# Graph network kernel: count units of 30 columns instead of 40, edge attributes copied to PSUM by ScalarE and summed from there, the last two stages begun with count group 0

## The reference

```python
# stages 0 and 1: edge attributes are used, batch norm follows
msg = relu(x[src] + edge_attr)                 # 100000 x 128
agg = segment_sum(msg, dst, num_segments=6250)
h = (x + agg) @ W1l + b1l
h = relu((h - mean(h)) * rsqrt(var(h) + 1e-5) * gl + bl)
x = relu(relu(h @ W2l + b2l))
# stages 2 and 3: no attributes
agg = segment_sum(x[src], dst, num_segments=6250)
h = relu(((1 + eps) * x + agg) @ wA.T + bA) @ wB.T + bB     # relu after stage 2 only
```

## Time and profile before

| what | before |
|---|---|
| median of 3 runs | 2944.27 us |
| profiled execution | 2942.28 us, span 2939.8 us |
| gathers of stage 0, first to last | 48.5 to 1063.0 us |
| gathers of stage 1 | 1117.6 to 2140.5 us |
| stage 2, first gather to first product of the perceptron | 2214.7 to 2547.9 us |
| stage 3, the same | 2580.8 to 2913.3 us |
| busy: PE, DVE, ACT, POOL | 1875.7, 1610.4, 519.3, 2024.0 us |

### The profile page before, as it was taken

How to read it: one execution, slowest core, us unless ns; L and a number is a source line. 1 busy time by engine, 2 the same in 40 slices (tenths; PEclk the granted TensorE clock), 3 DMA queues, 4 the chain that set the end, 5 groups by cost and what they waited for, 6 DMA issues and landing times.

```text
span 2939.8 us, 28632 instructions
## 1 busy us (share of the span) xinstructions
PE 1875.7 (64%) x9233; PEld 1286.7 (44%) x9233; DVE 1610.4 (55%) x1943; ACT 519.3 (18%) x584; POOL 2024.0 (69%) x2060
## 2 busy tenths in 40 slices
PE   2555465555555564565655555555566999969998
PEld 2434343444444342343434343344343566535665
DVE  6656666665666544666666666665654222342222
ACT  3111111111111222111222222222252000120001
POOL 3777777777777736777777777777706777267772
PEclk8777777777787777788788788988887999979999
DMA  5333333334343423344444444444405666266663
GB/s 166 101 114 109 114 111 105 122 100 128 108 130 110 133 75 109 124 135 122 137 133 139 130 140 136 161 138 154 128 28 189 215 216 215 81 198 205 217 217 100
DMA packets 224848, 403.61 MB, mean 137 GB/s; under 512 B 41225, under 2 KB 129117, under 8 KB 224741
## 3 DMA queue, kind: packets, MB, share of 16 engines
q1 hardware_dynamic: 159204, 267.94, 26.3%
q0 software_dynamic: 65536, 134.35, 17.0%
HBM read 337.92 MB, written 64.21 MB: 137 GB/s over the span
## 4 chain that ended last, share of the span: by engine, by line
POOL 53%; PE 24%; issue 17%; DVE 3%; DMA 1%; ACT 1%; SPq 1%; DVEq 0%; POOLq 0%; ACTq 0%
POOL xg L532 53%; PE psA L1210 16%; PE psG L1225 4%; PE psG L1274 2%; PE psA L1282 1%; DMA cell_room<-count_store 1%; DVE hid L927 0%; ACT rows_h L580 0%; PE psG L1189 0%; DVE xp_room L933 0%; SPq L411 0%; PE psG L1304 0%; PE psA L1291 0%; DVE xp_room L737 0%; DVE rows_h L766 0%
## 5 line engine op out<-in xcount | busy, mean ns | idle before, releaser
L532 POOL DMA_INDIRECT xg<-node_table,src_all x1568 | 1560.0, 995 | 576.6 <-issue 477.4
L1189 PE MATMUL psG<-hid,xp_room 128*128 128x160 f32 x3136 | 658.2, 389 | 793.3 <-DVE hid L820 793.3
L1189 PEld LDWEIGHTS psG<-hid,xp_room 128*128 128x128 f32 x3136 | 635.0, 265 | 836.6 <-issue 836.6
L552 POOL DMA_INDIRECT xg<-node_table,idx x480 | 460.9, 960 | 286.0 <-issue 275.4
L845 DVE TENSOR_SCALAR cell_room<-psG,cell_all 128x1960 f16<-128x1960 int16 x544 | 630.1, 1218 | 0.0
L856 DVE TENSOR_TENSOR xp_room<-xp_room,xg 128x1024 f32<-128x1024 f32 x196 | 238.7, 1218 | 670.4 <-DMA xg<-node_table,src_all 670.3
L1174 PE MATMUL psA<-cell_room,xp_room 128*128 128x512 f16 (+1 forms) x2176 | 478.4, 370 | 145.1 <-ACT count_out L590 145.1
L1174 PEld LDWEIGHTS psA<-cell_room,xp_room 128*128 128x128 f16 x2176 | 206.6, 98 | 386.4 <-ACT count_out L590 180.1
L590 ACT CAST count_out<-psA 128x1960 f16<-128x1960 f32 x96 | 172.0, 1792 | 960.6 <-PE psA L1174 960.6
L595 ACT ACTIVATE xp_room<-xp_room 128x1024 f32<-128x1024 f32 x196 | 206.3, 1057 | 722.2 <-DVE xp_room L856 721.8
L1210 PE MATMUL psA<-cell_room,xp_room 128*128 128x480 f16 x1200 | 248.9, 369 | 56.9 <-DMA cell_room<-count_store 56.9
(11 more groups left out here) (128 smaller groups left out, 611.6 us busy)
## 6 DMA issues: line engine op xcount, KB each, us to landing
xp_room<-in_edge_attr_dram SPq DMA_DIRECT2D x98, 768.0 KB, 4.7
cell_room<-count_store SPq DMA_DIRECT2D x16, 3000.0 KB
count_store<-count_out SPq DMA_DIRECT2D x96, 490.0 KB, 3.1
hid<-count_store SPq DMA_DIRECT2D x16, 2880.0 KB, 11.4
xp_room<-in_edge_attr_dram SPq DMA_DIRECT2D x98, 256.0 KB, 5.1
xg<-node_table,src_all POOLq DMA_INDIRECT x1568, 2.5
node_table<-rows_h SPq DMA_DIRECT2D x48, 256.0 KB, 2.3
xg<-node_table,idx POOLq DMA_INDIRECT x480
```

Of the source, the lines that this page charges most:

```text
L532: nc.gpsimd.indirect_dma_start(xg[:, n % 2, u, j, :], None, table, bass.IndirectOffsetOnAxis(ap=src_all[:, s, j:j + 1], axis=0),).then_inc ...
L552: nc.gpsimd.indirect_dma_start(xg[:, q, u, j, :], None, table, bass.IndirectOffsetOnAxis(ap=idx[:, q, u, j:j + 1], axis=0),).then_inc(row_ ...
L1189: last = nc.tensor.matmul(psG[:, q, h * WIN:(h + 1) * WIN], ea[:, t, u, j, :], hot[:, q, u, j, :], start=(u == slots[0] and j == 0), stop= ...
```

## The change

- `CW` is 30, with 0.8 in place of 0.9 in the rule that sizes the units. By `unit_sizes()` this gives 136 units (8 groups of 17) instead of 96; `cells` has 1470 columns, `psA` is used in three banks (512, 512, 446), a group's product has 17*30 = 510 columns. The ring of cells has eight entries.
- The freed bank of `psA` is `ea_stage`, room for one super's attributes (512 columns). ScalarE copies the attributes of each super there, and VectorE adds `xg` to them from there, super by super (four adds of 512 columns in a turn), writing to `ea` as before. ScalarE stages super i+1 once super i is summed.
- ScalarE's evictions of a turn (`units_out`) now stand between the ReLU of half 0 and the wait for super 2 of that turn; before, they stood ahead of both halves.
- Gathers count on a semaphore for each super.
- In stages 2 and 3 TensorE multiplies both halves of group 0 first, then window 0, and from there half 0 of the next group, window, half 1, window. VectorE and ScalarE follow that order. SyncE loads half 0 of group 0 ahead of the table's stores.

```diff
-CW = 40
+CW = 30
-            if NODES * (b * b - a * a) + 1 + 0.9 * sqrt((n + 1) * P) / degree > CW - 1:
+            if NODES * (b * b - a * a) + 1 + 0.8 * sqrt((n + 1) * P) / degree > CW - 1:
-UPG = 12
+UPG = 17
-CELL_RING = 6
+CELL_RING = 8
+        ea_stage = psA[:, 3, 0:EPP * D]
@@ sync
+            load_half(2, 0, 0)
+            store_table(2)
             load_counts(2)
+            load_half(3, 0, 0)
             store_table(3)
             load_counts(3)
@@ gpsimd
-                            pool.wait_ge(summed, (n - 2) * WINDOWS + h + 1)
+                            pool.wait_ge(summed, (n - 2) * SLOTS + HALVES[h][-1] + 1)
@@ scalar
+            def stage_attributes(i):
+                n, u = divmod(i, SLOTS)
+                if u == 0:
+                    act.wait_ge(ea_loaded[n % RING], 32 * (n // RING + 1))
+                act.copy(ea_stage, ea[:, n % RING, u, :, :].rearrange("p j d -> p (j d)")).then_inc(ea_staged, 1)
             def edges(layer):
+                act.wait_ge(cell_shift_ready, 1)
+                stage_attributes(layer * TURNS * SLOTS)
                 for n in range(layer * TURNS, (layer + 1) * TURNS):
                     t = n % RING
-                    for k in turn_units(n):
-                        ... (the eviction, now units_out)
-                    for h, slots in enumerate(HALVES):
+                    for slots in HALVES:
+                        for u in slots:
+                            i = n * SLOTS + u
+                            act.wait_ge(summed, i + 1)
+                            if i + 1 < (layer + 1) * TURNS * SLOTS:
+                                stage_attributes(i + 1)
                         half = ea[:, t, slots[0]:slots[-1] + 1, :, :].rearrange("p u j d -> p (u j d)")
-                        act.wait_ge(summed, n * WINDOWS + h + 1)
                         act.activation(half, half, ACT.Relu).then_inc(msg_ready, 1)
+                        if slots == HALVES[0]:
+                            units_out(n)
@@ vector
-                    dve.wait_ge(ea_loaded[n % RING], 32 * (n // RING + 1))
-                    for h, slots in enumerate(HALVES):
-                        half = ea[:, n % RING, slots[0]:slots[-1] + 1, :, :].rearrange("p u j d -> p (u j d)")
-                        dve.wait_ge(gathered[n % 2][h], 16 * EPP * len(slots) * (n // 2 + 1))
-                        nc.vector.tensor_tensor(half, half, xg[...two supers...], ALU.add).then_inc(summed, 1)
+                    for u in range(SLOTS):
+                        dve.wait_ge(ea_staged, n * SLOTS + u + 1)
+                        dve.wait_ge(gathered[n % 2][u], 16 * EPP * (n // 2 + 1))
+                        nc.vector.tensor_tensor(ea[:, n % RING, u, :, :].rearrange("p j d -> p (j d)"), ea_stage,
+                                                xg[:, n % 2, u, :, :].rearrange("p j d -> p (j d)"),
+                                                ALU.add).then_inc(summed, 1)
@@ tensor
             def counted_edges(layer):
+                multiply_counts(layer, 0, 0)
+                multiply_counts(layer, 0, 1)
+                late_windows(layer, 0, 0)
                 with pe.Fori(0, pairs) as k:
-                    multiply_counts(layer, k, 0)
-                    late_windows(layer, k, 0)
-                    multiply_counts(layer, k, 1)
+                    multiply_counts(layer, k + 1, 0)
                     late_windows(layer, k, 1)
-                multiply_counts(layer, pairs, 0)
-                multiply_counts(layer, pairs, 1)
-                late_windows(layer, pairs, 0)
+                    multiply_counts(layer, k + 1, 1)
+                    late_windows(layer, k + 1, 0)
```

More of the change, by code:

```diff
@@ L118 @@
 assert FIRST <= COUNTED < SUPERS and UNITS == KEPT and KEPT_TURNS % 2 == 1 and SKIP % 2 == 0
-assert CBANKS == 4 and UPG * CW <= 512 and HALF_B * UPG >= CELL_RING * BLOCKS // 2
+assert CBANKS == 3 and MOST_CHUNKS < CELL_RING and UPG * CW <= 512 and EPP * D == 512
 def group_blocks(g):
@@ L319, in gnn_kernel @@
         out_written = sem("out_written")
-        gathered = [[sem(f"gathered{q}_{h}") for h in range(WINDOWS)] for q in range(2)]
+        gathered = [[sem(f"gathered{q}_{u}") for u in range(SLOTS)] for q in range(2)]
+        ea_staged = sem("ea_staged")
         ea_loaded = [sem(f"ea_loaded{t}") for t in range(RING)]
@@ L459, in edges, with load_half @@
                         load_turn(n + RING)
-            def load_group(layer, k):
-                group = sp.snap(k * use).with_bounds(min_val=0, max_val=LEFT_PAIRS)
+            def load_half(layer, k, h):
+                group = 0 if isinstance(k, int) else sp.snap(k * use).with_bounds(min_val=0, max_val=LEFT_PAIRS)
                 n = sp.snap(k + groups_before(layer, pairs) + 1)
-                for h, b in ((0, slice(0, HALF_B * CW)), (1, slice(HALF_B * CW, CB))):
-                    sp.wait_ge(counts_used[h], n)
-                    sp.dma_start(counts[h][:, :, :],
-                                 count_store[bass.DynSlice(group * UPG, UPG), :, b].rearrange("s p c -> p s c")
-                                 ).then_inc(counts_loaded[h], 16)
+                b = (slice(0, HALF_B * CW), slice(HALF_B * CW, CB))[h]
+                sp.wait_ge(counts_used[h], n)
+                sp.dma_start(counts[h][:, :, :],
+                             count_store[bass.DynSlice(group * UPG, UPG), :, b].rearrange("s p c -> p s c")
+                             ).then_inc(counts_loaded[h], 16)
             def load_counts(layer):
                 sp.wait_ge(parts_ready, (layer - 1) * NSPLIT)
+                load_half(layer, 0, 1)
                 with sp.Fori(0, pairs) as k:
-                    load_group(layer, k)
-                load_group(layer, pairs)
+                    load_half(layer, k + 1, 0)
+                    load_half(layer, k + 1, 1)
             load_turn(0)
@@ L616, in next_indices, with product_out @@
                     act.copy(idx[:, q, :, :], src_all[:, bass.DynSlice(s, SLOTS), :]).then_inc(idx_ready[q], 1)
-                def product_out(k):
+                def product_out(k, adds):
                     g = act.snap(k + groups_before(layer, pairs))
                     act.wait_ge(counts_used[1], act.snap(g + 2))
-                    act.wait_ge(added, act.snap(k * pair_adds(rounds) + adds_before(layer, pairs, rounds) + 1))
+                    act.wait_ge(added, act.snap(adds + 1))
                     act.copy(product[:, :, :], psA[:, 0, 0:UPG * CW].rearrange("p (s c) -> p s c", s=UPG)
                              ).then_inc(products_out, 1)
+                before = act.snap(adds_before(layer, pairs, rounds) + 0 * rounds)
+                product_out(0, before)
                 with act.Fori(0, pairs) as k:
                     next_indices(k, 0)
-                    product_out(k)
                     next_indices(k, 1)
-                product_out(pairs)
+                    product_out(k + 1, act.snap(k * pair_adds(rounds) + rounds * WINDOWS + UPG + before))
             def split_features(layer):
@@ L851, in edges @@
                     count_cells(n)
-                    dve.wait_ge(ea_loaded[n % RING], 32 * (n // RING + 1))
-                    for h, slots in enumerate(HALVES):
-                        half = ea[:, n % RING, slots[0]:slots[-1] + 1, :, :].rearrange("p u j d -> p (u j d)")
-                        dve.wait_ge(gathered[n % 2][h], 16 * EPP * len(slots) * (n // 2 + 1))
-                        nc.vector.tensor_tensor(
-                            half, half, xg[:, n % 2, slots[0]:slots[-1] + 1, :, :].rearrange("p u j d -> p (u j d)"),
-                            ALU.add).then_inc(summed, 1)
+                    for u in range(SLOTS):
[4 more added lines that the diff above has]
+                                                ALU.add).then_inc(summed, 1)
                     edge_windows(layer, n)
@@ L910, in counted_edges @@
                 before = dve.snap(adds_before(layer, pairs, rounds) + 0 * rounds)
+                late_windows(layer, 0, 0)
                 with dve.Fori(0, pairs) as k:
-                    late_windows(layer, k, 0)
+                    add_units(layer, k, dve.snap(k * pair_adds(rounds) + rounds * WINDOWS + before))
                     late_windows(layer, k, 1)
-                    add_units(layer, k, dve.snap(k * pair_adds(rounds) + rounds * (2 * WINDOWS) + before))
-                late_windows(layer, pairs, 0)
+                    late_windows(layer, k + 1, 0)
                 end = dve.snap(pairs * pair_adds(rounds) + rounds * WINDOWS + before)
```

21 lines of the change are left out of this document (11 added, 10 removed).

## The result

The changed kernel takes 2985.49 us (median of 4 runs, 2984.41 to 2989.86) against 2943.47 us on the same chip: ratio 1.0147, 95% interval 1.0129 to 1.0164. It is 42.0 us slower; 16 were forecast. Its profiled execution took 2985.55 us, with a span of 2983.7 and a mean clock of 0.786.

What follows compares the result with a forecast made beforehand. GpSimd's gathers were taken to bound stages 0 and 1, TensorE stages 2 and 3. 2942.3 - 34.5 (stage 0) + 51.5 (stage 1) - 1.7 (stages 2, 3) = 2957.6, plus 2.0: 2960 us; 8-in-10 range 2897 to 2992.

Steps and rivals of the forecast that it cites:

- Matmuls have 510 columns: 0.2150 instead of 0.2025 us: Stages 2 and 3: each product matmul takes longer, +14.7 us for the 1176 in a stage.
- The hidden part of group 0: Stages 2 and 3: multiplying half 0 of group 0 early, while half 1 loads, hides 17.1 us.
- Seventeen adds of units: End of stages 2 and 3: 17 adds of units behind the last product instead of twelve, 1.7 us more.
- The freed GpSimd: Stages 0 and 1: adds from PSUM stop delaying gathers, -34.5 us in stage 0, up to -43.0 in stage 1.
- The loop: Stage 1: evictions, staging copy, add, one-hot and next window form a cycle; periods 17.2, 20.6, 22.8 us; +40.5 us.
- The clock: Stage 1: TensorE's pauses between evictions drop it to 1.2 GHz, +1.9 or +1.2 us a turn, +54 us.
- The upper bound of 78: Stage 1: cost of TensorE's lower clock if all count chunks between evictions are slow, +78 us.
- The loop at full clock: Rival, stage 1: same loop, but short bursts keep TensorE at 2.4 GHz; 2906 us, 25%.
- the loop doesn't bind: Rival, stage 1: room for two turns in `xg` takes up the lags; 2865 us, 8%.
- an unfreed GpSimd: Rival: four adds a turn still hold gathers, stage 0 stays at 1014.5 us, loop sets stage 1; 2994 us, 5%.

Runs made afterwards that it cites:

- lines_split: Changed kernel with matmul segments moved to other 16-byte offsets (half 0 on multiples, half 1 mostly 8 bytes past), giving wrong results: 3002.45 us.
- width_28_b: Changed kernel with count units of 28 columns instead of 30 (18 units a group, sizing factor 0.6): 2946.78 us.
- groups_as_before_b: Changed kernel with the order of stages 2 and 3 and their loads taken back to the kernel before: 3016.97 us.
- adds_from_sbuf: Changed kernel with the earlier two adds of 1024 columns, both operands in SBUF, no PSUM staging, evictions ahead of the ReLUs: 2943.40 us, ratio 1.0012.
- stage_in_sbuf_b: evict_late with ScalarE's copy of the attributes going to SBUF instead of PSUM, so adds read both operands from SBUF: 2923.76 us.
- pauses_filled: Changed kernel with useless matmuls on TensorE (22, then 10) while it waits for evictions between unit ends of a turn: 2939.72 us.
- evict_late: Changed kernel with ScalarE's evictions of a turn moved behind the copy of super 3: 2885.30 us, ratio 0.9815 to the kernel before.

## Why the prediction was right and wrong

**Direction right, size wrong.** Of the profiled span's +43.9 us the prediction had +15.3. Of the 28.6 missing, 23.5 are in stages 2 and 3, 8.1 in stage 1, -1.4 in stage 0 and -1.6 between the parts.

**The step that failed is the term "Matmuls have 510 columns: 0.2150 instead of 0.2025 us"** (+14.7 us a stage; measured over both stages 29.4 + 22.0). I took the row of 480 columns as a price per column. The 80-byte segments of before begin at multiples of 80 and fill their five pieces of 16 bytes. The 60-byte segments don't. Measured are 0.2201 us in half 0 and 0.2288 in half 1; over both stages (1200 and 1152 matmuls) that is 1200 x 0.0051 + 1152 x 0.0138 = 22.0 us more than forecast, of the 23.5. The column price itself held where every segment lies in four pieces: 0.2150 us in half 0 of lines_split. lines_split moved both halves as this says, width_28_b took the second time of half 1 away, and groups_as_before_b excludes the new order as its cause. The Trainium skill (SBUF — State Buffer, "Specifications (TRN2)") says that SBUF has lines of 16 bytes and that an access crossing to a new line pays a penalty. That agrees with half 1's two times; it does not give half 0's 0.2201, which stays open. The prediction did not weigh the pieces, and no row of before shows their price, since all its segments were aligned.

**The other terms of stages 2 and 3 held.** The hidden part of group 0 was worked out as 17.1 us a stage, 34.2 for two: measured 34.0. Half 0 began at 2243.03, 5.0 us ahead of the issue of half 1's load (6 forecast), with a cold start of 18.67 us (18). Seventeen adds of units took 5.36 us, where twelve took 3.87: +1.5, 1.7 forecast.

**The freed GpSimd: right, though other parts of the change would have given some of it.** -35.9 against -34.5 us in stage 0, and no gather that begins inside an add from PSUM is held. Narrow units and smaller, moved adds also shorten the gathers' excess, as adds_from_sbuf and stage_in_sbuf_b show; the prediction had given them no effect, and in the order of the steps above only 16.1 us are left for the operand's place. The Trainium skill (SBUF — State Buffer, "Who interferes with whom") infers that a tensor_tensor on two SBUF operands leaves descriptor making alone. For these gathers that does not hold: 1.25 us beside such an add, 0.94 without. What of a gather is held, the reading of its indices in SBUF or the writing of its descriptors, no run tells.

**The loop: every step was there, one of them too short.** In the turn shown the first add begins at S + 5.94 (5.95 forecast), the first eviction begins at S + 9.5 (9.6), the copy takes 0.59 (0.60), the eviction 1.38 (1.39). From the last add to the next window it is 6.01 us and not 5.62: the first window add now follows 1.74 us behind the start of the add instead of 1.35, although the add itself is half as long. At nearly full clock turns with two and three ends take 21.0 and 23.2 us, 20.6 and 22.8 forecast. These 0.4 us in some 35 turns would make about 14 (an estimate) of the 15.4 us by which the loop (55.9) exceeded the forecast (40.5). VectorE's idle time in them the profile calls "issue"; what it is stays open. The forecast's own sum has a slip of 0.6 us: the last two-end turn has five chunks, so it stands at 20.6 - 0.9 - 20.0 = -0.3 and not at -0.9.

**The clock: right in kind, too dear.** 43.8 us instead of 54. In the turn shown the first pause lasted 2.29 us (2.7 in the mean of the turns with three ends), where I had put 3.2; the burst behind it was still at full rate, and only the one behind the second pause was slow. I had let both be slow. Over the 17 turns with three ends, 23 of 85 steps were slow behind the first pause and all 95 behind the later ones; in the 23 turns with two ends it was 102 of 193 behind the first and 18 of 45 behind the second. The upper bound of 78, where the prediction put the rule of the Trainium skill on pauses between bursts (TensorE: Matmul & The Clock Gate, "Why this matters for your kernels"), is not what these turns show.

**Luck in stage 1.** Its miss of 8.1 us is smaller than its parts, because two of them cancel: the freed gathers gave 40.1 us and not 43.0 (+2.9), the loop cost 15.4 more, the clock 10.2 less. Each part carries the few us by which profiles differ.

**The rivals.** The loop at full clock comes to 2985.5 - 43.8 = 2941.7 us by pauses_filled, not 2906, since the loop and the matmuls were both mis-sized. That rival's condition was met in part: in turns with three ends 62 of 85 steps kept the full rate behind the first pause, and none behind the later ones. That the loop doesn't bind is excluded by 49 waiting gathers and by evict_late, and so is an unfreed GpSimd by gathers of 0.944 us.

## What to carry to other kernels

When a scarce engine is freed, ask what stands queued ahead of the work it now depends on: here an eviction queued ahead of a copy that another engine waits for closed a loop that cost 100 us, and moving it by one place brought all of that back. When segments of a strided matmul operand change their length, look at where they begin and end in 16-byte pieces, not only at the number of columns. A low clock costs time only on the path: with the evictions moved, more of the matmuls were slow than before and the kernel was 100 us faster.

## What the runs showed of the hardware

- A matmul of 510 fp16 columns in 17 segments of 60 bytes starts every 0.215 us if its segments lie in four pieces of 16 bytes and every 0.242 us if in five: 0.027 us for 17 more pieces, 1.6 ns each. Not every piece has that price: 480, 504 and 510 columns in 60, 72 and 68 pieces took 0.2025, 0.2125 and 0.2150, which is 0.42 ns a column. Where the segments of one matmul are mixed (half 0, rows of 1500 bytes) it is 0.2201, less than halfway; and 504 columns with mixed starts took 0.2151 against 0.2125 though none of their segments has a fifth piece. The pieces explain half 1, not these two.
- Count matmuls of 1.4 us a burst, with pauses of 1.5 us between them, ran at the 1.2 GHz level in the changed kernel from the second pause on in the turns with three ends (all 95 steps, granted clock 0.50 in the window shown); filling the pauses left 18 slow steps of 691.
- An add of 512 columns takes VectorE 0.67 to 0.69 us whether its second operand lies in SBUF or in PSUM; only the gathers beside it tell the difference: 1.100 us in the mean for those that begin inside it with both operands in SBUF, 0.945 with one in PSUM.
- ScalarE's copy of 512 float32 columns from SBUF to PSUM takes 0.59 us, as its copy from PSUM to SBUF did.
